# Mixture-of-experts layer: routed rows added to a table in memory by scattering transfers, and a last stage in 8 KB rows

## The reference

```
x1  = x + layernorm(attention(layernorm(x)))          # 16 query heads, 4 key heads, causal
xn  = layernorm(x1)
aff = sigmoid(xn @ wa)                                # 16 routed experts
p,i = top_k(aff, 2);  p = p / sum(p)
expert_e(v) = (gelu(v @ g_e + gb_e) * (v @ w1_e + b1_e)) @ w2_e + b2_e      # 512 -> 256 -> 512
z   = xn + sum over 2 shared experts + sum over the 2 chosen experts of p * expert
out = x1 + layernorm(z)
```

## Time and profile before

| | |
|---|---|
| time, median of 3 runs | 2229.0 us (2221.55 to 2233.6) |
| time of the profiled execution | 2223.3 us |
| its span | 2221.6 us |
| mean granted TensorE clock | 0.876 of full speed |
| busy: PE, DVE, ACT, POOL | 1782.6, 953.5, 560.7, 431.2 us |
| moved by DMA | 262.55 MB, mean 118 GB/s |
| the chain that ended last | PE 71%, DVE 8%, issue 7%, ACT 5%, POOL 5%, DMA 3% |

### The profile page before, as it was taken

One profiled execution on the slowest core, in us unless ns is written; L12 is line 12 of the kernel. 1 busy time (PEld: TensorE's weight loads), 2 busy tenths in 40 slices (PEclk: granted clock), 3 DMA queues, 4 the chain that ended last, 5 costly groups with the idle time before them and its releaser, 6 DMA issues.

```text
span 2221.6 us, 24135 instructions
## 1 busy us (share of the span) xinstructions
PE 1782.6 (80%) x7806; PEld 1031.0 (46%) x7807; DVE 953.5 (43%) x2127; ACT 560.7 (25%) x1119; POOL 431.2 (19%) x669
## 2 busy tenths in 40 slices
PE   4488888888888888886559999997999999999100
PEld 3354555545455555543336666664444444444000
DVE  2544555464646545463444222121233332332687
ACT  2133333342433333344231111111222222221000
POOL 1022121212222121222112111111111111111333
PEclk8588889888988888898769999998999999999555
DMA  3525244435534344433123333333344424431664
GB/s 113 65 65 92 73 122 94 126 91 114 129 80 118 76 124 81 107 88 132 69 92 124 132 130 133 133 125 128 110 166 165 163 91 138 143 111 66 222 227 170
DMA packets 120131, 262.55 MB, mean 118 GB/s; under 512 B 16092, under 2 KB 41694, under 8 KB 116200
## 3 DMA queue, kind: packets, MB, share of 16 engines
q1 hardware_dynamic: 108568, 223.39, 36.1%
q0 software_dynamic: 11440, 37.63, 4.5%
HBM read 248.50 MB, written 100.43 MB: 157 GB/s over the span
## 4 chain that ended last, share of the span: by engine, by line
PE 71%; DVE 8%; issue 7%; ACT 5%; POOL 5%; DMA 3%; SPq 1%; POOLq 0%; ACTq 0%; DVEq 0%
PE bank L1720 26%; PE bank L1929 12%; PE bank L1946 6%; PE bank L1824 4%; PE bank L1801 4%; PE bank L1827 3%; PE bank L1784 3%; POOL wr L1706 2%; PE bank L1919 2%; DVE tmp L1219 2%; PE bank L1933 2%; PE bank L1939 1%; PE bank L1911 1%; PE bank L1887 1%; PE bank L1907 1%
## 5 line engine op out<-in xcount | busy, mean ns | idle before, releaser
L1287 DVE TENSOR_REDUCE mx<-bank 128x1 f32<-128x512 f32 (+3 forms) x352 | 219.6, 635 | 208.9 <-PE bank L1786 208.1
L1042 ACT ACTIVATE P<-bank 128x512 f32<-128x512 f32 x320 | 190.6, 596 | 410.6 <-PE bank L1801 410.0
L1929 PE MATMUL bank<-ring,xg 128*128 x632 | 287.0, 597 | 0.0
L1784 PE MATMUL bank<-Ks,Qs 96*128 96x384 f32 (+3 forms) x512 | 167.7, 394 | 67.8 <-DVE mx L1287 36.8
L1720 PE MATMUL bank<-ws,xt 128*128 128x512 f32 x768 | 195.0, 403 | 12.7 <-DMA xt<-xt_scratch 12.7
L1801 PE MATMUL bank<-Qs,Ks 97*128 97x512 f32 x320 | 162.4, 508 | 42.7 <-ACT P L1042 36.6
L1720 PEld LDWEIGHTS bank<-ws,xt 128*128 128x128 f32 x768 | 140.2, 189 | 72.0 <-issue 30.7
L1929 PEld LDWEIGHTS bank<-ring,xg 128*128 128x128 f32 x632 | 115.0, 192 | 115.6 <-issue 115.6
L1701 POOL DMA_INDIRECT yt_scratch<-wst,idx x79 | 76.0, 962 | 444.9 <-DVE wst L1575 438.5
L1784 PEld LDWEIGHTS bank<-Ks,Qs 96*128 96x128 f32 x512 | 108.3, 229 | 109.8 <-DVE mx L1287 52.0
L1720 PE MATMUL bank<-wo_s,ynr 128*128 128x512 f32 x384 | 130.6, 466 | 35.4 <-DVE x L1346 23.9
(11 more groups left out here) (229 smaller groups left out, 2627.5 us busy)
## 6 DMA issues: line engine op xcount, KB each, us to landing
ring<-in_w SPq DMA_DIRECT2D x79, 1024.0 KB
ring<-in_w SPq DMA_DIRECT2D x79, 512.0 KB
Qs<-st SPq DMA_DIRECT2D x192, 128.0 KB, 4.6
xs<-xs_scratch SPq DMA_DIRECT2D x79, 258.0 KB
xs_scratch<-xs_scratch SPq DMA_DIRECT2D x78, 258.0 KB, 4.9
xt<-xt_scratch SPq DMA_DIRECT2D x32, 512.0 KB, 3.2
xs<-xn_scratch SPq DMA_DIRECT2D x64, 256.0 KB, 2.9
wr<-yt_scratch SPq DMA_DIRECT2D x64, 256.0 KB, 3.3
```

Of the source, the lines that this page charges most:

```text
L1042: e.activation(Pt[:, p, :], bank[PA.bank[step]][:, :], ACT.Exp, scale=SCALE).then_inc(s_exp, 1)
L1287: e.tensor_reduce(mx[:, G % 2, :].rearrange("p (h i) -> p h i", i=4)[:, h:h + n, i:i + 1], bank[PA.bank["max", b, p, j]][:, 0:n * k].rearr ...
L1784: e.matmul(ps[:, o * k:o * k + k], Qs[0:96, 4 * g + h + o, i * 128:(i + 1) * 128], Ks[0:96, b % 2, g, 0:k], start=o == 0, stop=False)
L1929: e.matmul(ps[:, :].rearrange("p (o n) -> p o n", o=1), xg[:, q, 128 * k:128 * k + 128], ring[:, bass.ds(reg[n], 1), 512 * k:512 * k + 512 ...
```

## The change

- The two-part table YT and the SBUF buffer acc are gone. A table Z in HBM has one row for each token and 128 rows for places without one. In "spread" of the shared stage SyncE writes each tile's sum to Z from a ring of three buffers zs (and once 128 rows more, so that the spare rows hold something finite).
- GpSimd's scatter of a routed tile becomes an adding transfer (compute_op add) into Z: the transfer reads the row in Z, adds, and writes it back. Both parts of a token go to the same row. GpSimd waits for the scatter of tile n-1 before it issues that of tile n.
- X1 is loaded into an SBUF buffer x1s (64 KB in each partition) during the routed stage, in 8 transfers of 1 MB.
- The last stage reads Z in 8 groups of four tiles, in transfers of 1 MB in which a partition gets 8 KB in one piece (four neighbouring tokens), into the memory of the weight ring. VectorE takes statistics of the four tiles, and one fused instruction for each tile does the scaling and the addition. GpSimd does four small operations for each group (reciprocal root of the variance, and the mean with its sign changed times that), ScalarE adds the bias to x1s. SyncE writes the output in half groups of 512 KB.

```diff
@@ shared stage, SyncE
                 elif kind == "spread":
+                    w.wait_ge(zs_dve, n + 1)
+                    if n == 0:
+                        e.dma_start(Z[NT * 128:NT * 128 + 128, :], zs[:, 0, :]).then_inc(d_zs[0], 16)
+                    e.dma_start(Z[128 * n:128 * n + 128, :], zs[:, n % 3, :]).then_inc(d_zs[n % 3], 16)
                     load_rows(n + 2)
@@ routed stage, SyncE
                     fetch_rows(n + 4)
+                    if n % 8 == 4 and n // 8 < NG:
+                        g = n // 8
+                        e.dma_start(group(x1s, g), X1_g[g]).then_inc(d_x1, 16)
@@ last stage, SyncE
-            def routed_over(): ...
-            def fetch(t): ...
+            w.wait_ge(rdown_pe, NS)
+            for i in range(8):
+                w.wait_ge(d_wr[i], 32 * len(range(i, NS, 8)))
+            for i in range(3):
+                w.wait_ge(d_ys[i], 16 * len(range(i, NS, 3)))
+            for g in range(NG):
+                e.dma_start(group(zf, g), Z_g[g]).then_inc(d_zg[g], 16)
+            for g in range(NG):
+                for h in range(2):
+                    w.wait_ge(f_out, 4 * g + 2 * h + 2)
+                    e.dma_start(out_g[g][:, 1024 * h:1024 * h + 1024], group(zf, g, 2 * h, 2 * h + 2)).then_inc(d_o, 16)
@@ ScalarE, after the routed stage
+            w.wait_ge(d_x1, 16 * NG)
+            for t in range(NT):
+                w.wait_ge(f_rs, t // 4 + 1)
+                e.activation(x1s[:, t, :], x1s[:, t, :], ACT.Identity, bias=nb3[:, t:t + 1]).then_inc(f_x1, 1)
@@ shared stage, VectorE
-                    e.tensor_tensor(acc[:, t, :], bank[PM.bank[step]][:, :], xs[:, s, 0, 0:512], ALU.add).then_inc(acc_dve, 1)
+                    if t >= 3:
+                        w.wait_ge(d_zs[t % 3], 16 * (t // 3 + (t % 3 == 0)))
+                    e.tensor_tensor(zs[:, t % 3, :], bank[PM.bank[step]][:, :], xs[:, s, 0, 0:512], ALU.add).then_inc(zs_dve, 1)
@@ last stage, VectorE (before: the six instructions of lines 1580 to 1593 for each tile)
+            def last(g):
+                for t in range(4 * g, 4 * g + 4):
+                    w.wait_ge(f_rs, g + 1)
+                    w.wait_ge(f_x1, t + 1)
+                    e.scalar_tensor_tensor(zf[:, t, :], zf[:, t, :], rs3[:, t:t + 1], x1s[:, t, :], ALU.mult, ALU.add).then_inc(f_out, 1)
+            for g in range(NG):
+                w.wait_ge(d_zg[g], 16)
+                for t in range(4 * g, 4 * g + 4):
+                    e.bn_stats(bst3[:, t, :], zf[:, t, :]).then_inc(dve_own, chain.up())
+                for t in range(4 * g, 4 * g + 4):
+                    w.wait_ge(dve_own, chain.n - 3 + t % 4)
+                    e.bn_aggr(mv3[:, t, :], bst3[:, t, :]).then_inc(f_mean, 1)
+                if g:
+                    last(g - 1)
+            last(NG - 1)
@@ routed stage, GpSimd
-                    e.indirect_dma_start(YT, bass.IndirectOffsetOnAxis(ap=idx[:, s:s + 1], axis=0), yo[:, o, :], None).then_inc(d_ys[o], 16)
+                    if n:
+                        w.wait_ge(d_ys[(n - 1) % 3], 16 * ((n - 1) // 3 + 1))
+                    else:
+                        for i in range(3):
+                            w.wait_ge(d_zs[i], 16 * (len(range(i, NT, 3)) + (i == 0)))
+                    e.indirect_dma_start(Z, bass.IndirectOffsetOnAxis(ap=idx[:, s:s + 1], axis=0), yo[:, o, :], None,
+                                         compute_op=ALU.add).then_inc(d_ys[o], 16)
@@ last stage, GpSimd (before: the addition of line 1706 and the power of line 1710 for each tile)
+            for g in range(NG):
+                c_ = slice(4 * g, 4 * g + 4)
+                w.wait_ge(f_mean, 4 * g + 4)
+                e.tensor_scalar(nb3[:, c_], mv3[:, c_, 1], EPS, None, ALU.add)
+                e.tensor_tensor(rs3[:, c_], nb3[:, c_], mhalf[:, :], ALU.pow)
+                e.tensor_scalar(nb3[:, c_], mv3[:, c_, 0], -1.0, None, ALU.mult)
+                e.tensor_tensor(nb3[:, c_], nb3[:, c_], rs3[:, c_], ALU.mult).then_inc(f_rs, 1)
```

More of the change, by code:

```diff
@@ L476, in program @@
     XS = nc.dram_tensor("xs_scratch", [NS * 128, XW], F32, kind="Internal").ap()
-    YT = nc.dram_tensor("yt_scratch", [2 * NT * 128 + NS * 128, D], F32, kind="Internal").ap()
+    Z = nc.dram_tensor("z_scratch", [NT * 128 + 128, D], F32, kind="Internal").ap()
     x_t = x.rearrange("b (i p) d -> (b i) p d", p=128)
-    out_t = out.rearrange("b (i p) d -> (b i) p d", p=128)
     PA, PM = plan_attention(), plan_moe()
@@ L605, in program @@
             ring = nc.alloc_sbuf_tensor_at("ring", [128, NSLOT, 3072], F32, offset=low + 12288)
-            acc = sb2("acc", [128, NT, 512])
+            x1s = sb2("x1s", [128, NT, 512])
             comb = sb2("comb", [128, NT, E])
@@ L630, in program @@
             one_b = sb2("one_b", [128, 128], BF16)
[L631 to L635, removed]
+            bst3 = sb2("bst3", [128, NT, 6])
+            mv3 = sb2("mv3", [128, NT, 2])
+            rs3 = sb2("rs3", [128, NT])
+            nb3 = sb2("nb3", [128, NT])
+        NG = NT // 4
         cmb2 = wr[:, 2, 0:NT * E].rearrange("p (t e) -> p t e", e=E)
@@ L638, in program, with group @@
         yo = wst[:, 0:1536].rearrange("p (a b) -> p a b", a=3)
-        zx = wr[:, :, :].rearrange("p a b -> p (a b)")[:, 0:NF * 3 * 512].rearrange("p (s k d) -> p s k d", s=NF, k=3)
-        YT_t = YT[0:2 * NT * 128, :].rearrange("(k i p) d -> k i p d", k=2, p=128)
+        zs = wst[:, 1536:3072].rearrange("p (a b) -> p a b", a=3)
+        zf = ring[:, :, :].rearrange("p a b -> p (a b)")[:, 0:NT * 512].rearrange("p (t d) -> p t d", t=NT)
+        Z_g = Z[0:NT * 128, :].rearrange("(g p i) d -> g p (i d)", g=NG, p=128)
+        X1_g = X1.rearrange("t p d -> (t p) d").rearrange("(g p i) d -> g p (i d)", g=NG, p=128)
+        out_g = out.rearrange("b t d -> (b t) d").rearrange("(g p i) d -> g p (i d)", g=NG, p=128)
+        def group(v, g, lo=0, hi=4):
+            return v[:, 4 * g + lo:4 * g + hi, :].rearrange("p t d -> p (t d)")
         comb_dve, wd_pool, m_dve, up_pool = sem("comb_dve"), sem("wd_pool"), sem("m_dve"), sem("up_pool")
@@ L648, in program @@
         turn_pe, hT_hi, hT_lo = sem("turn_pe"), sem("hT_hi"), sem("hT_lo")
-        cT_pe, cT_act, down_pe, acc_dve, row_dve = sem("cT_pe"), sem("cT_act"), sem("down_pe"), sem("acc_dve"), sem("row_dve")
+        cT_pe, cT_act, down_pe, zs_dve, row_dve = sem("cT_pe"), sem("cT_act"), sem("down_pe"), sem("zs_dve"), sem("row_dve")
+        d_zs, d_x1 = sems("d_zs", 3), sem("d_x1")
         d_wr, d_xr2, d_ys = sems("d_wr", 8), sems("d_xr2", 4), sems("d_ys", 3)
@@ L674, in bank_free @@
                 w.wait_ge(sem_, PA.nth[(reader, *(was[1:3] if was[0] == "wo" else was[1:]))])
-        moe_read_by = {"up": h_dve, "turn": hT_lo, "cT": cT_act, "out": acc_dve, "take": xg_act, "rup": rh_dve,
+        moe_read_by = {"up": h_dve, "turn": hT_lo, "cT": cT_act, "out": zs_dve, "take": xg_act, "rup": rh_dve,
                        "rturn": hr_act, "rdown": yo_dve}
@@ L685, in moe_bank_free @@
             elif was[0] == "out":
-                w.wait_ge(acc_dve, was[1] + 1)
+                w.wait_ge(zs_dve, was[1] + 1)
             else:
@@ L887, in load_rows @@
                         w.wait_ge(d_sc[s], 32 * (t // 2))
-                        w.wait_ge(acc_dve, t - 1)
+                        w.wait_ge(zs_dve, t - 1)
                     for n in range(2):
@@ L901, in fetch_rows @@
                         w.wait_ge(down_pe, SH * NT)
-                        w.wait_ge(acc_dve, NT)
+                        w.wait_ge(zs_dve, NT)
                         w.wait_ge(d_sc[0], 16 * NT)
@@ L937, in _ @@
                     fetch_rows(n + 4)
+                    if n % 8 == 4 and n // 8 < NG:
+                        g = n // 8
+                        e.dma_start(group(x1s, g), X1_g[g]).then_inc(d_x1, 16)
                 elif kind == "rdown":
                     fetch_w(n + NSLOT)
[L941 to L967, removed]
+            w.wait_ge(rdown_pe, NS)
[9 more added lines that the diff above has]
+                    e.dma_start(out_g[g][:, 1024 * h:1024 * h + 1024], group(zf, g, 2 * h, 2 * h + 2)).then_inc(d_o, 16)
+            e.wait_ge(d_o, 16 * 2 * NG)
         @block.scalar
@@ L1700, in _ @@
                     w.wait_ge(idx_dve, n + 1)
-                    e.indirect_dma_start(YT, bass.IndirectOffsetOnAxis(ap=idx[:, s:s + 1], axis=0), yo[:, o, :], None).then_inc(d_ys[o], 16)
[L1703 to L1710, removed]
+                    if n:
[8 more added lines that the diff above has]
+                w.wait_ge(f_mean, 4 * g + 4)
+                e.tensor_scalar(nb3[:, c_], mv3[:, c_, 1], EPS, None, ALU.add).then_inc(pool_own, chain.up())
+                w.wait_ge(pool_own, chain.n)
+                e.tensor_tensor(rs3[:, c_], nb3[:, c_], mhalf[:, :], ALU.pow).then_inc(pool_own, chain.up())
+                w.wait_ge(pool_own, chain.n)
```

(3 more changed lines are left out.)

9 lines of the change are left out of this document (4 added, 5 removed).

## The result

The changed kernel takes 2244.14 us (median of 6 runs, 2237.12 to 2245.88) against 2227.62 us before (6 runs): a ratio of 1.0068 with a 95% interval of 1.0046 to 1.0091. It is slower, by a little, where the prediction had it 1.4% faster. The last stage gave back more than was forecast; the routed stage took more than that.

What follows compares the result with a forecast made beforehand. The prediction took TensorE to bound the shared and routed stages, and a serial VectorE and GpSimd pass the last. Its terms, -89.6 + 51.8 + 6.5 = -31.3 us, gave 2195 us, range 2135 to 2265 (8 in 10).

Steps and rivals of the forecast that it cites:

- D: Time by which an adding scatter is longer than a plain one, issue to landing: taken as 1.5 us, range 0 to 2.9.
- the slack: Routed stage: VectorE's idle time for TensorE, 0.92 us a tile, 68.7 us in all, which a longer scatter could use up.
- The sign given for a D above 0.9: Profile after, routed stage: VectorE's idle time for TensorE ahead of the scaling would be gone.
- second rival: Routed stage: the adding scatter becomes the bound and outweighs the last stage's gain; 2301 to 2307 us at D = 2.9; chance 0.22.
- Its formula: Whole kernel: last stage, routed stage and drain summed, 78D - 148.3 us against the kernel before.
- Routed stage: The stage grows by 75D + 8 - 68.7 us if that is positive; 51.8 us with D = 1.5.
- The 8 us for the X1 loads: Routed stage: the 8 MB of added X1 loads cost VectorE 8 us of its slack, about 1 us a MB.
- Last stage: From the last scatter's landing to the end: 67.2 us in place of 156.8, a gain of 89.6 us, VectorE the bound.
- The rival of a transfer-bound last stage: Last stage: transfers limit it, 79 us in place of 61, 18 us less gain, about 2213 us; chance 0.06.
- Drain: End of the routed stage: the last three scatters land one after another, a loss of 2.0 + 3D, 6.5 us.
- Up to the routed stage: Shared stage: 33 more stores of 256 KB and a wait on SyncE, covered by TensorE, taken as 0.
- The balance: Whole kernel: gain against loss, 78D - 148.3 us, so slower from D = 1.9 on.

Runs made afterwards that it cites:

- e6: The changed kernel with adding scatters moving rows of 1 KB in place of 2 KB, half of each routed row left out: 2173.56 us, one run.
- e7: The changed kernel with plain scatters of 1 KB rows, the addition and half of each routed row left out: 2129.76 us, one run.
- e9: The changed kernel with the last nine weight loads left out, later experts computed with others' weights: 2215.28 us, ratio 0.9947 to the kernel before.
- e1: The changed kernel with eight columns for weight and place in place of four, so VectorE waits for the scatter of tile n-8: 2140.84 us, ratio 0.9607.
- e2: The changed kernel with plain scatters in place of adding ones, so each row overwrites: 2130.51 us, ratio 0.9559.
- e4: The kernel before the change, with eight columns in place of four: 2227.19 us, ratio 0.9993.
- e3: The changed kernel with the eight 1 MB X1 loads moved from the routed stage into the shared stage: 2245.18 us, ratio 1.007.

## Why the prediction was wrong

**What failed is the term D, the price of an adding scatter over a plain one.** It stood at 1.5 us, as 0.7 for a second stream of bytes and 0.8 for the read's round trip. Measured it is 2.03 in an undisturbed tile (about 1.30 by bytes, 0.59 GpSimd's issue, 0.14 left, by e6 and e7) and 2.48 in the mean of all (443.1 - 257.1 over 75). The other 0.45 are mostly the weight loads, whose price the prediction had carried over unchanged: spread over some 15 loads, the waits of the kernel before are 1.6 us above the undisturbed one for each load, and those of the changed kernel 3.9 (58 us above the undisturbed 5.13 in 75 tiles); e9 gave back 3.3 for each load left out. GpSimd's issue was named in the prediction as a cost without a row, and then entered at nothing in the value taken. A first guess was at hand: half of the plain issue's 0.96 us once more, for the destination's read, would have been an estimate of 0.48, near the 0.59 measured.

**The mechanism held.** VectorE stands still for the scatter that it has just fed, the slack was 0.92 us, and the surplus fell on the stage. e1 takes the wait away and the stage returns to 488.6 us; e2 takes the adding away and the same happens; e4 shows that the wait was free before. The sign given for a D above 0.9, no idle time ahead of the scaling, came as well. This is the prediction's second rival, "the adding scatter becomes the bound and costs more than the last stage gives", which had a chance of 0.22 and was to decide from D = 1.9 on.

**Its formula, with the measured D of 2.48, gives +45 us; the spans differ by +20.** That would be 2268 us and more, above the range's end of 2265 (D = 2.4). That the range still held the 2244 us measured is luck in part: the last stage and the stage's formula each erred to the other side. Term by term:

- Routed stage: 75 x 2.48 + 8 - 68.7 = 125 by the formula, 107.9 measured. The 8 us for the X1 loads weren't there (e3). Most of the remaining 9 should be that VectorE's instructions start up to 0.1 us earlier when one follows directly on the other (line 1580 starts 0.35 us after the start of a 0.42 us one in the timeline above); that is read off, not tested.
- Last stage: -89.6 forecast, -104.3 measured. VectorE was the bound, as taken, but at 1.32 us a tile, not 1.72: four statistics in a row take 2.38 us and four fused instructions 2.62 (0.60 and 0.66 each, where one alone lasts 0.69 and 0.74), so independent instructions overlap at their ends. I had added the durations of instructions that wait for one another. At 32 tiles that is 12.8 us, of which 10.9 reach VectorE's whole stretch (44.2 us from its first statistics to its end), since it also waits 1.6 us for ScalarE. Most of the rest is the end: 3.1 us after VectorE's last instruction, where I had 6.7 (5.7 of before, and 1.0 for the larger transfer). The rival of a transfer-bound last stage is out: the stage moved 323 GB/s, and VectorE hardly waited after the first group had landed. That group took 4.97 us, below my 5.4. It is also below the 6.15 us that the Trainium skill ("DMA: Bandwidth & Descriptors", section Bandwidth) has for a load of 1 MB issued from GpSimd; here SyncE issues it, and the measurement decides.
- Drain: 2.0 + 3D, which is 6.5 at 1.5 and 8.1 at 2.03, against 11.4. Left out were the 0.69 us between one landing and the next issue, three times, since the scatter of tile 76 has to wait for that of tile 75 too; that is 2.1 of the 3.3 us that are missing at 2.03.
- Up to the routed stage: 0 forecast, +5.4 measured; the shared stage alone, from its first sum to its last, has +6.1 (371.0 to 377.1). e1 and e2 have +3.6 there, and e4, with the code of before, +0.4. All of it lies in tiles 2 to 4, where the plan catches up with the scatters it had to hold for the routing; from the fifth tile on the period is 12.13 us in each of these kernels. Some cost is real, then, 3 to 6 us. Which of the added steps it is wasn't tried.

**What to expect of a forecast like this.** The balance hung on D 78 times, and two rows far apart (0 and 2.9) bounded it. The value in it was taken too near to the favourable end: 1.5, where the mean measured was 2.48.

## What to carry to other kernels

A transfer that an engine waits for directly after feeding it is in that engine's loop, hidden or not: read its slack off the timeline before making it heavier. Here the wait was there for four columns of indices, cost nothing in the old kernel, and was worth 103 us once the scatter grew by 2 us. When a change fails on such a wait, lengthen the ring before dropping the change: with eight columns the same change is 4% faster than the kernel before.

To price a new kind of transfer, count its issue on the issuing engine, its bytes, and what it meets on the queues; and price a run of independent instructions by the distance of their starts, not by their durations.

## What the runs showed of the hardware that I had not expected

- An adding scatter of 128 rows costs 0.96 us for each KB of row length where a plain one costs 0.31, and GpSimd needs 1.55 us to issue it in place of 0.96, at 1 KB and at 2 KB rows alike. It is moved in 144 packets at either size, the plain one in 80 or 48.
- A 1.5 MB load issued just after an adding scatter delays its landing by 3 to 4 us (3.9 by the mean of fifteen, 3.3 by leaving nine out). The plain scatters of the kernel before lost 1.6 us for each such load, though not each load fell beside one.
- In the last stage, 1 MB loads with 8 KB in each partition ran at up to 435 GB/s in single stretches, where the last stage of the kernel before had 349 at most in 256 KB transfers:

```profile
GB/s 63 334 429 416 429 416 429 435 435 416 429 422 410 435 422 328 221 384 435 413 413 432 416 413 309 13 391 391 25 0 359 394 54 0 337 391 79 312 391 104
```

The row is the rate in 40 equal slices from 2190 to 2242 us of the changed kernel.
